# Two-layer graph network: the low halves of the layer 1 probabilities are made, and transposed, in another order

## What is computed

```python
# layer 0
h = relu(layernorm(x))
q, k, v = heads(h @ Wq + bq), heads(h @ Wk + bk), heads(h @ Wv + bv)      # 6 heads of 128
probs = softmax(q @ k.T / sqrt(128) + where(adj, 0, -9e15))
x = x + (probs @ v) @ Wf + bf
# layer 1
h = relu(layernorm(x))
g = einsum('bnd,ade->bane', h, W); th = tanh(g)                            # 12 heads of 64
attn = leaky(th @ w_src + (th @ w_dst).T, 0.2)
attn = softmax(where(adj, attn, -999))
out = elu(attn @ g + b)
gate = sigmoid(h @ H_w.T + H_b)
x = x + gate * out + (1 - gate) * h
```

## Time and profile before

| | |
|---|---|
| median of 3 runs | 2726.34 us (2725.95 to 2729.07) |
| profiled execution | 2724.92 us, its span 2723.1 us |
| mean granted TensorE clock | 0.961 of full speed |
| PE busy | 2499.8 us, 92% |
| DVE busy | 2142.5 us, 79% |
| ACT busy | 994.9 us, 37% |
| POOL busy | 785.0 us, 29% |
| 16 DMA engines, by their queue's packets | 48.7% of the span |

### The profile page before, as it was taken

How to read it: one execution, slowest core, us unless ns; L and a number is a source line. 1 busy time by engine, 2 the same in 40 slices (tenths; PEclk the granted TensorE clock), 3 DMA queues, 4 the chain that set the end, 5 groups by cost and what they waited for, 6 DMA issues and landing times.

```text
span 2723.1 us, 56736 instructions
## 1 busy us (share of the span) xinstructions
PE 2499.8 (92%) x22691; PEld 1777.9 (65%) x22691; DVE 2142.5 (79%) x3100; ACT 994.9 (37%) x1295; POOL 785.0 (29%) x562
## 2 busy tenths in 40 slices
PE   7999999999999999999999999999999999999997
PEld 5666666666666666666666666666666666666665
DVE  7877877778877788777787777887777877778868
ACT  6433333333333233333333333433323333333334
POOL 1232233222331332322223312233222232222322
PEclk9999999999999999999999999999999999999999
DMA  7464545454554544454444545354554545444442
GB/s 239 122 141 103 128 119 127 110 120 103 130 116 123 126 95 127 112 130 120 100 123 127 119 120 124 92 130 113 128 121 99 128 115 130 114 111 112 127 105 48
DMA packets 603273, 325.09 MB, mean 119 GB/s; under 512 B 515808, under 2 KB 532704, under 8 KB 603232
## 3 DMA queue, kind: packets, MB, share of 16 engines
q1 hardware_dynamic: 603232, 324.50, 48.7%
HBM read 172.60 MB, written 29.88 MB: 74 GB/s over the span
## 4 chain that ended last, share of the span: by engine, by line
PE 59%; DVE 16%; DMA 8%; issue 7%; SPq 6%; ACT 2%; DVEq 0%; POOL 0%; ACTq 0%; POOLq 0%
PE pair_prj L752 40%; PE pair_prj L776 8%; PE pair_prj L1030 5%; DMA p_place<-arena 4%; DMA arena<-arena 4%; SPq L590 3%; SPq L596 3%; PE pair_att L792 2%; DVE p_place L1553 2%; DVE bn_out L1213 2%; DVE max L1577 2%; PE pair_att L875 2%; DVE arena L1492 2%; ACT h_hi L1875 1%; DVE arena L1257 1%
## 5 line engine op out<-in xcount | busy, mean ns | idle before, releaser
L752 PE MATMUL pair_prj<-w_hi,arena 128*128 128x512 f16 (+1 forms) x4776 | 1121.0, 325 | 3.6 <-DVE arena L1448 2.1
L752 PE MATMUL pair_prj<-w_lo,arena 128*128 128x512 f16 (+1 forms) x2388 | 776.7, 325 | 0.0
L752 PEld LDWEIGHTS pair_prj<-w_hi,arena 128*128 128x128 f16 x4776 | 467.4, 98 | 309.5 <-DVE arena L1448 2.4
L776 PE MATMUL pair_prj<-arena,w_hi 128*128 128x256 f16 x2376 | 428.7, 287 | 3.1 <-DVE arena L1257 2.3
L2242 POOL TENSOR_TENSOR rstd<-var_eps,minus_half 128x2 f32<-128x2 f32 x62 | 62.2, 1002 | 1044.5 <-DVE var_eps L1226 1037.5
L776 PE MATMUL pair_att<-arena,w_hi 128*128 128x256 f16 x2160 | 356.9, 273 | 0.0
L776 PE MATMUL pair_prj<-arena,w_lo 128*128 128x256 f16 x1188 | 339.6, 286 | 0.0
L752 PEld LDWEIGHTS pair_prj<-w_lo,arena 128*128 128x128 f16 x2388 | 233.9, 98 | 148.1 <-issue 0.7
L776 PE MATMUL pair_att<-arena,w_lo 128*128 128x256 f16 x1080 | 294.4, 273 | 0.0
L776 PEld LDWEIGHTS pair_prj<-arena,w_hi 128*128 128x128 f16 x2376 | 240.6, 103 | 41.8 <-DVE arena L1257 2.9
L1875 ACT ACTIVATE h_hi<-arena,shift,rstd 128x768 f16<-128x768 f32 x124 | 120.6, 1019 | 382.0 <-DVE shift L1231 382.0
(11 more groups left out here) (244 smaller groups left out, 4363.7 us busy)
## 6 DMA issues: line engine op xcount, KB each, us to landing
w_hi<-forms SPq DMA_DIRECT2D x179, 288.0 KB, 4.3
w_lo<-forms SPq DMA_DIRECT2D x179, 288.0 KB, 4.8
arena<-in_x SPq DMA_DIRECT2D x63, 768.0 KB, 4.3
out<-arena SPq DMA_DIRECT2D x64, 384.0 KB, 2.3
arena<-arena SPq DMA_TRANSPOSE x372, 3.3
arena<-in_L_gnn_Wq SPq DMA_DIRECT2D x2, 1152.0 KB, 7.8
arena<-in_L_gnn_Wk SPq DMA_DIRECT2D x2, 1152.0 KB, 11.8
w_hi<-in_L_gnn_Wv SPq DMA_DIRECT2D x2, 1152.0 KB, 12.3
```

The costliest lines, as they stand in the source:

```text
L752: mm = nc.tensor.matmul(pair[:, lo:hi], lhs(a, k), weight(m, k, b)[:, lo:hi], start=(k == 0 and n == 0), stop=(k == KT - 1 and n == 2))
L776: mm = nc.tensor.matmul(pair[:, c * 256:(c + 1) * 256], weight(m, k, a)[:, o:o + P], (ht0_hi, ht0_lo)[b][:, k, :], start=(k == 0 and n == ...
```

## The change

Four edits, in two engines' lists. On SP, lo(1) with its two waits goes ahead of the high rows of layer 1. On DVE, from i = 3 on, `p1_low(1, p)` goes from the head of the iteration to behind the statistics of x1 (before the sum of tile 1); i = 2, where `carried` is false, keeps the old place. At the end of groups 2 to 30, add_form 3 goes ahead of low_sums(0, 3), add_form 4 into the place between tile 0's maximum and subtraction, and `p1_low(0, j)` goes ahead of tile 1's maximum. No instruction is added or taken away.

```diff
@@ SP, one() @@
                     after_held(sp, transposes_held, p1_hi_made, 2 * p + 2)
                     after_held(sp, transposes_held, sum1_ready, 2 * p + 1)
                     transpose_blocks(pt1[1][0], e1[0], pt1_hi_landed[1])
+                    after_held(sp, transposes_held, p1_lo_made, 2 * p + 2)
+                    after_held(sp, transposes_held, sum1_ready, 2 * p + 2)
+                    transpose_blocks(pt1[1][1], e1[1], pt1_lo_landed[1])
                 if mid:
                     if isinstance(j, int) and j == 0:
                         sp.wait_ge(weight_ready, made_ready(WG, 1))
                     else:
                         after_held(sp, transposes_held, g_psum, 2 * j)
                     transpose_rows(1, 0, ht1_hi, j)
-                if last:
-                    after_held(sp, transposes_held, p1_lo_made, 2 * p + 2)
-                    after_held(sp, transposes_held, sum1_ready, 2 * p + 2)
-                    transpose_blocks(pt1[1][1], e1[1], pt1_lo_landed[1])
                 if mid:
                     transpose_rows(1, 1, ht1_lo, j)
@@ DVE, one() @@
-                if last:
+                if last and not carried:
                     p1_low(1, p)
                 if now:
                     dve.wait_ge(q_psum, 2 * i + 1)
...
                     dve.wait_ge(x1_ready, f_before(j) + f_parts(j))
                     variance(1, x1, j)
+                    p1_low(1, p)
...
                     leak_and_mask(0, lambda: add_form(i, 2))
+                    add_form(i, 3)
                     low_sums(0, 3)
-                    shift1(0, lambda: add_form(i, 3))
-                    add_form(i, 4)
+                    shift1(0, lambda: add_form(i, 4))
                     leak_and_mask(1, lambda: add_form(i, 5))
                     low_sums(3, 4)
+                    p1_low(0, j)
                     shift1(1)
-                    p1_low(0, j)
                     sum_and_invert(0, j)
```

## The result

The changed kernel takes 2575.8 us (median of 4 runs, 2575.1 to 2576.5) against 2727.4 us before (4 runs): a ratio of 0.9444, 95% interval 0.9428 to 0.9460, 152 us less. 2561 was forecast, 2510 to 2632 the range. The profiled execution took 2575.38 us, 149.5 less than that of before, which is 5.16 us in each of 29 iterations where 5.7 were forecast.

The account below looks back on a forecast made before the run. PE's idle time ahead of attend(1) was taken as the bound: 7.0 us recoverable, 5.7 after DVE's limit, less 0.5 for collision, plus 0.5 for clock. 5.7 in 29 iterations, 165 us, gives 2561 us; range 2510 to 2632.

Parts of the forecast that it names:

- The loop through DVE, DMA, ACT and SP: Ahead of attend(1): this loop makes tile 1's transposes late; cutting it moves shift 2.6 us earlier and removes 5.5 idle.
- The clock, 1.5 us and 0.5 on the average: PE behind attend(1)'s stall: 1.5 us lost at low clock in the iteration shown, 0.5 more on average.
- Edit 3: DVE's iteration end, p1_low(0) earlier, add_form(3) and low_sums(0,3) exchanged: nothing once p1_low(1) has moved, alone 1.0 us.
- PE held back by low_values(1) ahead of H1: PE at project_h's second tile: could start at 1294.2, starts at 1295.5, leaving 5.7 of the 7.0 us.
- The wait of output_min(1) for POOL's bias: DVE behind output_first(1): output_min(1) must newly wait for POOL's bias, so it starts 5.1 us earlier.
- the collision behind H1: DVE's low parts against POOL's first product: a tie costing 0 to 1.1 us, taken as 0.5.
- A: Rival: DVE doesn't hold PE back, PE saves 7.6 us an iteration, 220 in all: 2505 us; 8%.
- B: Rival: shift not earlier, from DVE's loop turn or POOL's power colliding with p1_low(1); attend(1) awaits query bias: 2630; 15%.
- C: Rival: idle time only changes its name, lo(1) still lands at 1273 as sum(1) is late; within 0.2%; 3%.
- D: Rival: short PE stalls at 1246 and ahead of H1 lower its clock; slower, 2790 at 16 us; 4%.
- Those for "right": Signs: line 792's wait under 10 us, no 0.5 clock, SP's new order, PE waiting 1 to 1.5 us ahead of H1.
- The one for a collision: Sign of being wrong: low parts and products (L1253, L2303) longer by over 1 us each.

Follow-up runs that it names:

- run 1: The changed kernel with SP's old order, the high rows ahead of lo(1) again: 2624.9 us, ratio 0.9625.
- run 2: The kernel before with the edit on SP alone, lo(1) ahead of the high rows, DVE's order as it was: 2669.5 us, ratio 0.979.
- run 3: The changed kernel with p1_low(0) back behind tile 1's shift: 2577.8 us, ratio 0.9454.
- run 4: The changed kernel with add_form 3 and 4 and low_sums(0,3) in the old order: 2576.3 us, ratio 0.9448.
- run 5: The kernel before with only p1_low(0) ahead of the maximum and add_form 3 and low_sums(0,3) exchanged: 2698.6 us, ratio 0.9896.
- Run 6: The changed kernel, layer 0's low parts in the loop replaced by DVE instructions of equal length with one PSUM operand: 2545.0 us, ratio 0.9333.
- run 7: The changed kernel with tile 1's low and high values ahead of the softmax's sum on DVE and exponential on ACT: 2664.2 us, ratio 0.978.
- run 8: The changed kernel with h_low(0) ahead of layer 0's two low parts on DVE: 2555.3 us, ratio 0.937.

## Why the prediction was right, point by point
- **The loop through DVE, DMA, ACT and SP, cut by the two main edits: right.** The wait at attend(1) went from 169 us to under 1, DVE's wait for tile 0's transposes vanished, the high rows no longer stand in front of lo(1), and shift came 2.8 us earlier (2.6 forecast, with 0.55 for DVE's loop turn, which took 0.16). Runs 1 and 2 show that each edit alone leaves 49 to 94 us behind.
- **The clock, 1.5 us and 0.5 on the average: right.** No stretch of attend(1) is at 1.2 GHz now, mean clock 0.997, PE busy 55 us less, which is 1.9 us in each of 29. The iteration that was worked through is not typical: in 27 of the 29 the low level lasted about twice as long as in it (windows), and the 0.5 added for that was needed.
- **Edit 3 worth nothing here, 1.0 alone: right** (runs 3, 4 and 5: 2 us, 0.6 us, 28 us). The 1.0 of run 5 is in part luck: DVE's wait shrank by 0.7, and some 0.4 came from the clock, which the forecast did not have.
- **PE held back by low_values(1) ahead of H1: right in kind**, 1.73 us instead of 1.3. **The wait of output_min(1) for POOL's bias** came too, 1.0 us.
- **The term that was too small is the collision behind H1.** The forecast took 0.5 us, the middle between a won tie, 0, and a lost one, 1.1, which is also what it had by the Trainium skill's rule alone (SBUF — State Buffer, "Who interferes with whom"). It counted POOL's delay alone. But POOL won the tie, and the loss came all the same, since DVE is delayed as well: both low parts are hit, the pair goes from 3.44 to 5.07, h_low(0) and h_target(0) come late, and PE waits 0.75 at the gate. Run 6, without the collision, is 31 us faster, 1.1 an iteration. Taking the whole of it instead of 0.5 would have moved the forecast by 17 us, to 2578, 2 from the measured median. That the two 1.1 agree is chance: the forecast's is the delay of POOL's second products, run 6's is the price of the whole collision, which the kernel before had in a milder form.
- **Rivals.** A (2505, DVE doesn't hold PE back) is out by the 1.73 us ahead of H1. B (2630) is out for the changed kernel, whose shift is earlier; its place, attend(1) waiting for the query bias, is just what run 2 shows, with 2.0 us and 2669, 40 us above B's price, in which there was no collision, and no low clock ahead of H1 (41 us in run 2). One of B's two causes did come: p1_low(1) now starts with POOL's power, which takes 1.50 us instead of 0.70 (the 23 us of line 2242; one iteration before and one after, below). It costs nothing, since DVE has the sum to make before shift needs the power, and p1_low(1) itself still takes 0.96. C is out by SP's issues. D did not happen here: behind all 28 waits ahead of H1, 1.3 to 2.0 us, the clock stayed full. But it was near. Waits of 2.3 us in the same place brought it in run 2, and run 7 shows what it costs at 3.3. The forecast went by 0.96 and 5.5 us alone; in the first iterations of the kernel before, the clock fell behind three of the four waits of 1.9 to 2.3 us (those ending at 63.5, 73.9 and 101.9, not that at 44.9). So that D stayed away is in part luck.
- **The signs.** Those for "right" came, but for the size of the wait ahead of H1 (1.73 us, not 1 to 1.5). The one for a collision, over 1 us on each low part and product, was set too wide: the low parts grew by 0.8 each and the first product not at all, and that was the miss.

```profile
1262.34 0.70 POOL L2242 TENSOR_TENSOR rstd<-var_eps,minus_half 128x2 f32<-128x2 f32 x1 [29.04 <-DVE var_eps L1226]
```
```profile
1275.39 1.50 POOL L2242 TENSOR_TENSOR rstd<-var_eps,minus_half 128x2 f32<-128x2 f32 x1 [25.01 <-DVE var_eps L1225]
```

## What to carry to other kernels
Find the whole loop that sets the pace, across engines and queues, before moving a step: here the same edit was worth 28 us with one wait in front and nothing with another, and two edits needed each other. Once a loop is cut, ask which instructions now run at the same time that didn't before; two engines that exclude each other are both late, and all that stands behind either in its list. Don't merge short waits of TensorE into a long one: beside two of 1.7 and 0.75 us, one of 3.3 us cost 88 us in a kernel of 2576. And look at the mean granted clock of every run: in run 2 the median matmul of the step in question looked well, while 41 us went at the low clock 28 us further on.

## What the runs showed of the hardware
- TensorE's granted clock kept its full level behind all 28 idle times of 1.3 to 2.0 us ahead of H1 in the changed kernel; in runs 6 and 8 it fell behind 2 of 28 each (2.0 to 2.1 us). In run 2 it fell behind 3 of 29 of 1.5 to 2.2 us at attend(1), and behind 21 of 25 of 2.3 us ahead of H1. Behind 3.0 to 3.7 us in run 7 it fell in 24 of 28 cases (behind one of 3.2 it was 0.50 over the next 5.2 us); behind 3.28 us in run 1 it held for attend(1) and averaged 0.71 over the 5.9 us from its start; behind 5.5 us it was 0.50, then 0.91.
- A DVE instruction with two SBUF operands and a POOL instruction that reads SBUF took turns whole: a pair of 0.95 us each took 5.07 us on DVE, and 1.8 became 2.5 on POOL. With one of the DVE operands in PSUM neither was stretched.
- A DVE loop turn cost 0.16 us of idle time, against 0.75 us between the end of SP's last issue of one iteration and the first of the next in the kernel before.
